# Making the tile tables of six token groups on GpSimd instead of VectorE, in an attention and mixture-of-experts block

## What is computed

```python
u  = zX * lap_x(x) + zY * lap_y(x) + zR * x * (1 - x)          # neighbours along both axes
hn = layernorm(u, ln1); q, k, v = split(hn @ in_proj.T + b)    # 16 heads of 16
x1 = u + softmax(causal(q k / 4)) v @ out_proj.T + b           # attention over the 16 positions
hn2 = layernorm(x1, ln2)                                       # 4096 tokens of 256
rp = softmax(hn2 @ router_w.T); top 2 of 8 experts             # gates are the two probabilities
y  = sum over the two experts: gelu(hn2 @ w1[e]) @ w2[e] * gate
out = x + x1 + y
```

## Time and profile before

| | |
|---|---|
| median of three runs | 682.89 us (678.2 to 685.67) |
| the profiled execution: its own time | 681.01 us |
| its span, first to last instruction | 679.3 us |
| TensorE busy | 585.8 us (86%) |
| VectorE busy | 441.9 us (65%), 1031 instructions |
| GpSimd busy | 430.7 us (63%), 502 instructions |
| ScalarE busy | 360.5 us (53%) |
| granted TensorE clock, mean | 0.952 |

### The profile page before, as it was taken

How to read it: one execution, slowest core, us unless ns; L and a number is a source line. 1 busy time by engine, 2 the same in 40 slices (tenths; PEclk the granted TensorE clock), 3 DMA queues, 4 the chain that set the end, 5 groups by cost and what they waited for, 6 DMA issues and landing times.

```text
span 679.3 us, 10489 instructions
## 1 busy us (share of the span) xinstructions
PE 585.8 (86%) x2808; PEld 415.5 (61%) x2808; DVE 441.9 (65%) x1031; ACT 360.5 (53%) x827; POOL 430.7 (63%) x502
## 2 busy tenths in 40 slices
PE   2579979898479988998989997999878999999992
PEld 2346656666357656666666764667556676666661
DVE  1267659788989999998968799969973500111110
ACT  4434452276346674664767675556534755444440
POOL 5877654854884487767788658860784584544442
PEclk9979998699799998998999999999989999999997
DMA  5476853431251232334234323441344455444332
GB/s 134 132 235 202 239 177 92 114 87 32 87 104 40 47 104 41 59 59 95 67 75 99 70 27 86 74 71 31 73 94 71 71 114 79 65 73 69 64 48 23
DMA packets 51547, 59.84 MB, mean 88 GB/s; under 512 B 7386, under 2 KB 47075, under 8 KB 51428
## 3 DMA queue, kind: packets, MB, share of 16 engines
q0 software_dynamic: 18288, 23.28, 21.2%
q1 hardware_dynamic: 33204, 35.91, 18.4%
HBM read 35.89 MB, written 27.46 MB: 93 GB/s over the span
## 4 chain that ended last, share of the span: by engine, by line
PE 41%; DVE 26%; POOL 14%; issue 7%; DMA 6%; ACT 4%; SPq 1%; POOLq 0%; DVEq 0%; ACTq 0%
PE b_y L996 11%; PE b_h L981 10%; DVE qk_prod L859 7%; DVE sc L867 6%; DVE pv_prod L927 5%; POOL xs_d L435 5%; DMA out_dram<-y,xin 3%; PE b_at L1140 3%; PE b_qk L1094 3%; PE b_t L988 3%; PE b_at L1087 2%; POOL out_dram L470 2%; PE b_x L972 2%; PE b_v L1094 2%; DMA xin<-xs_d 1%
## 5 line engine op out<-in xcount | busy, mean ns | idle before, releaser
L470 POOL DMA_INDIRECT out_dram<-y,xin x71 | 123.7, 1743 | 30.5 <-issue 22.2
L996 PE MATMUL b_y<-w_s,hm_hmT 128*128 x568 | 138.9, 389 | 3.3 <-ACT y L569 1.9
L981 PE MATMUL b_h<-w_s,xT 128*128 x284 | 134.0, 594 | 0.3
L996 PEld LDWEIGHTS b_y<-w_s,hm_hmT 128*128 128x128 f32 x568 | 105.1, 195 | 18.4 <-issue 6.4
L1140 PE MATMUL b_at<-ident,pv_prod 128*128 128x128 f32 x544 | 76.9, 295 | 29.1 <-DVE pv_prod L927 28.9
L859 DVE TENSOR_TENSOR qk_prod<-q,kv 128x1024 f32<-128x1024 f32 (+2 forms) x80 | 90.8, 1159 | 0.8
L1140 PEld LDWEIGHTS b_at<-ident,pv_prod 128*128 128x128 f32 x544 | 66.9, 153 | 37.3 <-issue 28.2
L927 DVE TENSOR_TENSOR pv_prod<-kv,pr 128x1024 f32<-128x1024 f32 (+2 forms) x80 | 87.2, 1135 | 2.6 <-PE b_at L1140 1.4
L694 DVE TENSOR_SCALAR y<-b_y,xin,live 128x256 f32<-128x256 f32 x24 | 13.1, 544 | 112.8 <-PE b_y L996 102.1
L435 POOL DMA_INDIRECT xs_d<-ring,slot_row x64 | 72.0, 1124 | 18.9 <-issue 18.6
L867 DVE TENSOR_REDUCE sc<-qk_prod 128x64 f32<-128x1024 f32 (+2 forms) x80 | 82.1, 1050 | 0.3
(11 more groups left out here) (170 smaller groups left out, 1085.2 us busy)
## 6 DMA issues: line engine op xcount, KB each, us to landing
xin<-xs_d SPq DMA_DIRECT2D x71, 132.5 KB, 2.2
w_s<-in_L_ffn_w_dram SPq DMA_DIRECT2D x16, 512.0 KB, 4.4
xp<-in_x_dram SPq DMA_DIRECT2D x32, 128.0 KB
xud<-in_x_dram SPq DMA_DIRECT2D x32, 128.0 KB
out_dram<-x POOLq DMA_DIRECT2D x32, 128.0 KB, 3.2
xud<-in_x_dram SPq DMA_DIRECT2D x32, 126.0 KB
out_dram<-y,xin POOLq DMA_INDIRECT x71, 3.9
xud<-in_x_dram SPq DMA_DIRECT2D x64, 1.0 KB
```

The costliest lines, as they stand in the source:

```text
L470: pool.indirect_dma_start(out_rows, bass.IndirectOffsetOnAxis(ap=xin[:, j % NX, H:H + 1].bitcast(U32), axis=0), y[:, j % NY, :], None, com ...
L981: mm = pe.matmul(b_h[:, :], xT[:, k * P:(k + 1) * P], w1_s[:, bass.ds(e * (HC * F) + k * F, F)], start=(k == 0), stop=(k == HC - 1))
L996: mm = pe.matmul(b_y[:, 0:H], hmT[:, k * P:(k + 1) * P], w2_s[:, bass.ds(e * (FC * H) + k * H, H)], start=(k == 0), stop=(k == FC - 1))
```

## The change

GpSimd makes the tables of groups 0 to 5. VectorE only leaves the number of full tiles per expert in `smalli`, with two more instructions at the end of `route_slots`, and its `route_tiles` is called for the last group alone (`route_last_tiles`). GpSimd's `route_tiles(r)` stands in step `ROUTE + 2`, behind the group's last scatters and behind the fillers, ahead of `diffuse`. A running sum over 8 experts, which VectorE did with a scan, takes three rounds of copy and shifted addition there, and sums over experts are done by halving.

```diff
+            def route_tiles(r):                                   # on GpSimd
+                a, b = FIRST[r], FIRST[r + 1]
+                m, rows = b - a, tabr[:, a:b]
+                pool.wait_ge(s["slots_ready"], r + 1)
+                link(pool.tensor_copy(full, smalli[:, :]))
+                link(pool.tensor_tensor(full, full, done[:, 0:E], ALU.subtract))
+                for by in (1, 2, 4):
+                    src, dst = (full, d8) if by != 2 else (d8, full)
+                    pool.tensor_copy(dst[:, 0:by], src[:, 0:by])
+                    link(pool.tensor_tensor(dst[:, by:E], src[:, by:E], src[:, 0:E - by], ALU.add))
+                link(pool.tensor_scalar(acc[:, 1:E + 1], d8, float(m), None, ALU.min))
+                link(pool.tensor_tensor(full, done[:, 0:E], acc[:, 0:E], ALU.subtract))
+                pool.tensor_tensor(done[:, 0:E], full, acc[:, 1:E + 1], ALU.add)
...
+                link(pool.tensor_scalar(rows, tf[:, 1, 0:m], s8[:, 0:1], None, ALU.add))
+                if r == 0:
+                    pool.tensor_copy(tab[:, a:b], tf[:, 0, 0:m]).then_inc(s["tab_ready"], 1)
+                else:
+                    pool.tensor_copy(tab[:, a:b], tf[:, 0, 0:m])
+                    link(pool.tensor_tensor(apart[:, 0:m], tabr[:, a:b], tabr[:, a - 1:b - 1], ALU.subtract))
+                    link(pool.tensor_scalar(apart[:, 0:m], apart[:, 0:m], P, -16, ALU.is_equal, ALU.mult))
+                    pool.tensor_tensor(tabw[:, a:b], apart[:, 0:m], tabw[:, a:b], ALU.add).then_inc(s["tab_ready"], 1)
@@ GpSimd's loop @@
                 if g in PREFIX:
                     prefix(PREFIX.index(g))
+                if g - 2 in ROUTE:
+                    route_tiles(ROUTE[g - 2])
                 if g + AHEAD + 1 < G:
                     diffuse(g + AHEAD + 1)
@@ VectorE, route_slots @@
                 link(dve.tensor_tensor(base[:, 0:E], base[:, 0:E], tot, ALU.add))
+                if r < NG - 1:
+                    if r >= 1:
+                        dve.wait_ge(s["tab_ready"], r)
+                    link(dve.tensor_tensor(smalli[:, :], base[:, 0:E], ebase, ALU.subtract))
+                    link(dve.tensor_scalar(smalli[:, :], smalli[:, :], 7, None, ALU.arith_shift_right))
@@ VectorE's loop @@
                 if g in ROUTE:
                     counted(ROUTE[g])
                     route_slots(ROUTE[g])
-                if g - 1 in ROUTE:
-                    route_tiles(ROUTE[g - 1])
...
-            route_tiles(NG - 1)
+            route_last_tiles()
```

More of the change, by code:

```diff
@@ L229, in adaln_moe_block @@
         TAIL = FIRST[NG - 1]
+        base, done, acc, top_of, s8, l8 = [rs[:, 16 * i:16 * i + E + 1] for i in range(6)]
+        cnt, full, d8 = [rs[:, 96 + 8 * i:104 + 8 * i] for i in range(3)]
         def projected_late(g):
@@ L446, in prefix, with spread @@
                                             zrow, None).then_inc(s["pre_done"], 16)
+            def spread(col, n, m):
+                return col.rearrange("p (n o) -> p n o", o=1).to_broadcast([P, n, m])
+            def route_tiles(r):
[11 more added lines that the diff above has]
+                pool.tensor_tensor(done[:, 0:E], full, acc[:, 1:E + 1], ALU.add)
+                pool.tensor_tensor(tt[:, 0, 0:m, 0:E - 1], spread(iota_t[:, 0:m], m, E - 1),
+                                   acc[:, 1:E].rearrange("p (o e) -> p o e", o=1).to_broadcast([P, m, E - 1]), ALU.subtract)
+                link(pool.tensor_scalar(s8[:, 0:E], full, float(P), None, ALU.mult))
+                link(pool.tensor_tensor(s8[:, 0:E], s8[:, 0:E], ebase, ALU.add))
+                link(pool.tensor_scalar(tt[:, 0, 0:m, 0:E - 1], tt[:, 0, 0:m, 0:E - 1], 0.0, None, ALU.is_ge))
+                link(pool.tensor_tensor(d8[:, 0:E - 1], s8[:, 1:E], s8[:, 0:E - 1], ALU.subtract))
+                link(pool.tensor_tensor(tt[:, 1, 0:m, 0:E - 1], tt[:, 0, 0:m, 0:E - 1],
+                                        d8[:, 0:E - 1].rearrange("p (o e) -> p o e", o=1).to_broadcast([P, m, E - 1]), ALU.mult))
+                pool.tensor_scalar(tf[:, 2, 0:m], iota_t[:, 0:m], float(P), None, ALU.mult)
+                both = tt[:, :, 0:m, :]
+                link(pool.tensor_tensor(both[:, :, :, 0:3], both[:, :, :, 0:3], both[:, :, :, 4:7], ALU.add))
+                link(pool.tensor_tensor(both[:, :, :, 0:2], both[:, :, :, 0:2], both[:, :, :, 2:4], ALU.add))
+                link(pool.tensor_tensor(tf[:, 0:2, 0:m], both[:, :, :, 0:1].rearrange("p k m o -> p k (m o)"),
+                                        both[:, :, :, 1:2].rearrange("p k m o -> p k (m o)"), ALU.add))
+                link(pool.tensor_tensor(tf[:, 1, 0:m], tf[:, 1, 0:m], tf[:, 2, 0:m], ALU.add))
+                link(pool.tensor_scalar(rows, tf[:, 1, 0:m], s8[:, 0:1], None, ALU.add))
[6 more added lines that the diff above has]
+                    pool.tensor_tensor(tabw[:, a:b], apart[:, 0:m], tabw[:, a:b], ALU.add).then_inc(s["tab_ready"], 1)
@@ L721, in route_a @@
                                   top8[:, g0:g0 + n, 0:1].to_broadcast([P, n, E]), ALU.subtract).then_inc(s["rt_sub"], 1)
-            base, done, acc, top_of, s8, l8 = [rs[:, 16 * i:16 * i + E + 1] for i in range(6)]
-            cnt, full, d8, col = [rs[:, 96 + 8 * i:104 + 8 * i] for i in range(4)]
+            col = rs[:, 120:128]
             def counted(r):
@@ L800, in route_tiles @@
                                               op0=ALU.mult, op1=ALU.add))
[L801 to L815, removed]
@@ L816, in route_tiles @@
-                need(te)
[L817 to L828, removed]
+                link(dve.tensor_scalar(tf[:, 1, 0:m], tf[:, 1, 0:m], s8[:, 0:1], None, ALU.add))
@@ new lines, in route_last_tiles @@
+                link(dve.tensor_scalar(l8[:, 0:E], base[:, 0:E], float(P), None, ALU.subtract))
+                link(dve.tensor_tensor(d8[:, 0:E - 1], l8[:, 1:E], l8[:, 0:E - 1], ALU.subtract))
+                link(dve.tensor_tensor(tt[:, 1, 0:m, 0:E - 1], tt[:, 0, 0:m, 0:E - 1],
+                                       d8[:, 0:E - 1].rearrange("p (o e) -> p o e", o=1).to_broadcast([P, m, E - 1]), ALU.mult))
+                link(dve.tensor_reduce(tf[:, 2, 0:m], tt[:, 1, 0:m, 0:E - 1], AX, ALU.add))
@@ new lines, in route_last_tiles @@
+                link(dve.tensor_scalar(tf[:, 2, 0:m], tf[:, 2, 0:m], l8[:, 0:1], None, ALU.add))
+                link(dve.tensor_tensor(tf[:, 2, 0:m], tf[:, 2, 0:m], tf[:, 1, 0:m], ALU.min))
+                a, b = FIRST[r], FIRST[r + 1]
+                rows_made = tick(dve.tensor_copy(tabr[:, a:b], tf[:, 2, 0:m]))
+                link(dve.tensor_tensor(tf[:, 1, 0:m], tf[:, 1, 0:m], tf[:, 2, 0:m], ALU.subtract))
+                dve.tensor_scalar(live[:, 0:m], tf[:, 1, 0:m], iota_p, None, ALU.is_le)
@@ L830, in _ @@
+                need(te)
+                dve.tensor_copy(tab[:, a:b], tf[:, 0, 0:m])
+                need(rows_made)
+                link(dve.tensor_tensor(apart[:, 0:m], tabr[:, a:b], tabr[:, a - 1:b - 1], ALU.subtract))
+                link(dve.tensor_scalar(apart[:, 0:m], apart[:, 0:m], P, -16, ALU.is_equal, ALU.mult))
+                dve.tensor_tensor(tabw[:, a:b], apart[:, 0:m], tabw[:, a:b], ALU.add).then_inc(s["tab_ready"], 1)
             for g in range(-AHEAD, G + 3):
```

21 lines of the change are left out of this document (10 added, 11 removed).

## The result

The changed kernel takes **735.7 us** (median of 4 runs, 734.66 to 738.33), the kernel before beside it 682.58 us (4 runs). The ratio is 1.0791, with a 95% interval of 1.0749 to 1.0833. The profiled execution has a span of 736.6 us against 679.3; at 738.33 us it is the slowest of the four, so the two traces lie 57.3 us apart where the medians lie 53.1.

The account below looks back on a forecast made before the run. GpSimd's queue was taken to bound the scatter steps. Losses of 4.6 + 8.1 + 0.4 + 8.0 + 11.7 + 6.0 + 1.1 = 39.9 us on 681.0 gave 720.9, left at 721 us; range 691 to 742.

Parts of the forecast that it names:

- What bounds, and the sign: Scatter steps: GpSimd already late, VectorE early, waiting 15.1 us for `rstd`; slower by more than one per cent: 0.89.
- What GpSimd's table costs: GpSimd's 27 instructions (24 in group 0): 11.7 us in groups 1, 2, 4, 5; 9.5 in group 3; 8.5 in group 0.
- the estimate was 13.4 us: GpSimd's table, if six VectorE products a step each hold one instruction 1.0 us on average; some 8 us more in all.
- What of it shows, groups 1, 3, 4 and 5: Steps 13, 22, 27, 31: losses of 8.1, 8.0, 11.7 and 6.0 us through `rstd`, tile 19, tile 29 and tile 37.
- What of it shows, group 2: Step 17: VectorE 3.9 us earlier, but GpSimd's `rstd` only at 279.3, so the gain is eaten: +0.4 us.
- The sentence on what is moved past the table: Behind the tables in GpSimd's queue: `diffuse` and SyncE's loads of x both have over a step in hand.
- Group 0: Step 9: `rstd` 8.5 us late, less 3.9 us of VectorE waits no longer needed: 4.6 us; first tiles do not wait.
- The cheap chain: Rival: GpSimd's tables take 5.1 us a group with no hold; 8.7 us lost, 690 us; chance 0.12.
- VectorE as the bound: Rival: every table taken off VectorE counts, 22.8 - 2.4 = 20.4 us gained, 661 us; chance 0.06.
- Held throughout: Rival: GpSimd's table instructions held throughout, 17.6 us a table (11.7 in group 0); 75 us lost, 756 us; chance 0.07.
- That it does not show: Rival: TensorE or ScalarE so near behind the chain that gain and loss vanish, 681 to 683 us; chance 0.03.
- the signs named: Changed profile: instructions 0.3 to 0.45 us apart, tables 8 to 13 us, longer `rstd` and tile waits, nothing regained behind 520 us.

Follow-up runs that it names:

- the table in time: Kernel before, VectorE making all tables as before, GpSimd running the same 27 instructions on scratch data at the six places: 734.17 us, ratio 1.0777.
- the late table alone: Kernel before, VectorE making all tables, but tab_ready raised only in step ROUTE + 3 by one 0.2 us GpSimd instruction: 700.27 us, ratio 1.0295.

## Why the prediction was right or wrong

**What bounds, and the sign: right.** In the scatter steps GpSimd was the late engine and VectorE the early one. VectorE's relief is there, 23.3 us of busy time against 22.8 - 2.4 = 20.4 predicted, and shows as dips of 3.4 to 5.0 us in its steps. It is given back by longer waits: 6.25 us for `rstd` at step 14, 4.61 at step 28, 4.79 for TensorE in step 17.

**What GpSimd's table costs: right.** Predicted 8.5 + 4 x 11.7 + 9.5 = 64.8 us for six tables, measured 62.3. The 0.31 us for a linked pair holds (median of the six tables 0.315), and the addition of 4.3 us for held instructions is near the 3.9 to 4.5 us read off in group 2. By the rule of the Trainium skill (SBUF — State Buffer, "Who interferes with whom") the estimate was 13.4 us. The trace agrees with the rule, since all three held instructions end with the product they met; the chain met fewer products than that estimate had.

**What of it shows, groups 1, 3, 4 and 5: right in size, and the path right in two of them.** 8.1, 8.0, 11.7 and 6.0 us predicted, 9.0, 7.5, 13.2 and 6.4 measured. At group 3 the path is the predicted one, table to the load of tile 19, with `rstd` as late beside it; so is it at group 4, table to addition to tile load. At group 1 the prediction named only `rstd`; in the changed kernel TensorE waits 16.07 us for tile 3, and VectorE only 1.89 us for `rstd` behind the table. With the table in time that stop is 7.75 us and the group loses 7.9, with the late table alone 5.2: two gates of much the same length, of which the prediction saw the one that did not come last. At group 5 it had tile 37 wait for the addition; TensorE took tile 37 at 573.55 without a wait, and the loss comes by VectorE's stop of 6.35 us for `rstd`, which the prediction did not price there. That the sizes fit at groups 1 and 5 is in part luck.

**What of it shows, group 2: the step that failed.** It said that VectorE's 3.9 us would be eaten and the group cost +0.4. It followed only `rstd`, and 9.4 us were lost, though VectorE's next normalization did not wait for `rstd` at all: the stop of 11.11 us for TensorE, ahead of it, was the longer one. The table's first user, tile 11, was not looked at: its load had landed 3.3 us before TensorE took it in the kernel before (264.55 and 267.87), and now TensorE waited 7.36 us. Nor was the addition of tile 6, which stands behind the table and `diffuse` and on which tile 12's load waits; that load had 2.6 us to spare before (270.38 and 272.98). A late table alone costs this group 4.9 us, a late queue alone 7.1. The sentence on what is moved past the table named `diffuse` and the loads of x, and left out these additions.

**Group 0: the same omission, and a credit that did not come.** "Its first tiles come later, and do not wait" is wrong: tile 0 is taken in step 10, and waited 12.34 us. 4.6 us predicted, 8.5 measured. The delay of `rstd` itself was as foreseen, with a stop of 7.39 us. But the 3.9 us that VectorE was to save in that step by waiting no longer for ScalarE and TensorE were not saved; both stops are still there:

```profile
158.20 0.17 DVE L747 MAX8 top<-logits 128x8 f32<-128x8 f32 x1 [2.19 <-ACT logits L681]
...
163.26 0.20 DVE L776 COPY sums<-b_v 128x40 f32<-128x40 f32 x1 [1.75 <-PE b_v L1091]
```

With the table in time they are 0.60 and 1.72 us and the group loses 6.6, so the late queue alone passes the 4.6 as well.

**The rest.** These two groups make 12.9 of the 14.0 us between the two sums, and the forecast of 721 was 14.7 us low. Nothing is regained behind the groups: from step 34 to the end it took 157 us before and 159 after, as predicted.

**The rivals.** The cheap chain (5.1 us a table) falls by the tables' lengths, 7.7 us and more. VectorE as the bound (661 us) falls: its tables went away and the time did not. Beside that rival stood the remark of the Trainium skill (Perfetto Trace Analysis, "Optimizing Scalar/DVE Operations") that moving work between these two engines may not help because of the shared port. The trace agrees that it did not help, but holds are not why: one step earlier the tables took 9.1 to 11.2 us, much as here, and cost 11 us in all; the place in the queue is what cost. Held throughout (17.6 us a table) falls, since no table took over 12.3 us. The reason given, that VectorE soon stands still, is not what group 2 shows: VectorE worked on through the table there, but behind its product that ended at 285.64 it ran reductions and shorter products, and no instruction of the table took over 0.46 us. That it does not show falls by 53 us. Of the signs named, start-to-start times of 0.3 us and tables of 8 to 13 us (7.7 to 12.3) came. The waits at tiles 19 and 29 were to rise by about 8 and 12 us and rose by 5.8 and 9.5, to 8.07 and 11.17. Of the stops of 6 to 9 us behind groups 0, 1 and 3 only the first came as said (7.39, 1.89 and 10.26 us). VectorE's wait for `rstd` rose by 46 us in all, more than the 25 expected, and waits at tiles 0, 3, 11 and 12 were not foreseen.

## What to carry to other kernels

When work moves to an engine with a strict queue, list everything that stands behind its new place and everyone who waits for each of these, as well as for the moved result; a wait that is zero today is not a slack. Where two gates run side by side, taking one away proves little: here a late queue alone cost as much as late queue and late tables together, with VectorE's relief counted in. Look for the place where the receiving engine waits for the giving one: there the same 27 instructions cost a fifth, though in this kernel even that was a loss.

## What the runs showed of the hardware

Standing still costs TensorE again afterwards. The table of stretches (us, busy us of PE, PEld, DVE, ACT, POOL with counts, granted clock, DMA share, GB/s) around the 16 us wait for tile 3:

```profile
192.00:199.00 7.00, 6.69 (x26) 4.42 (x24) 0.87 (x3) 3.67 (x9) 5.82 (x7) 0.84 0.23 80
199.00:215.00 16.00, 0.04 (x1) 0.00 (x0) 11.81 (x19) 0.95 (x3) 13.77 (x33) 0.56 0.18 25
215.00:219.00 4.00, 3.88 (x11) 2.64 (x12) 0.41 (x3) 1.68 (x5) 3.67 (x6) 0.50 0.81 192
219.00:223.00 4.00, 4.00 (x21) 2.87 (x20) 3.92 (x5) 2.40 (x6) 0.98 (x2) 0.68 0.56 110
223.00:231.00 8.00, 8.00 (x35) 5.19 (x34) 6.65 (x14) 6.38 (x14) 6.25 (x9) 1.00 0.19 57
```

The granted clock fell to 0.50 (1.2 GHz) while TensorE stood, and came back to 1.00 (2.4 GHz) only behind 219. The four `b_h` products at 216.79 took 3.78 us; they took 1.98 us at 195.80 in the trace before, where the granted clock was 1.00 from 194 to 198. Over the whole kernel TensorE's busy time rose by 13.1 us, though it has the same matrix products to do. How much of that lies on the path was not measured.
